# Setup, scatter table and first prologue merged into the first attention block, the atoms' products in its second slot of scores

## What is computed

```python
x = x + tanh(g_xattn[0]) * rope_cross_attention(layernorm(x), ctx)      # 32 heads of 16
x = x + tanh(g_ffn[0])   * mixture_of_16_experts(layernorm(x))          # top 4
x = x + tanh(g_xattn[1]) * normed_cross_attention(layernorm(x), ctx)
x = x + tanh(g_ffn[1])   * sparse_delta_layer(layernorm(x))             # W and 8 deltas, top 2
```

## Time and profile before

| | us |
|---|---|
| median of 3 runs | 2079.18 (2077.33 to 2079.27) |
| the profiled execution | 2078.01 |
| its span in the trace | 2076.2 |
| mean granted clock of TensorE, as a share of 2.4 GHz | 0.953 |

### The profile page before, as it was taken

One profiled execution on the slowest core, in us unless ns is written; L12 is line 12 of the kernel. 1 busy time (PEld: TensorE's weight loads), 2 busy tenths in 40 slices (PEclk: granted clock), 3 DMA queues, 4 the chain that ended last, 5 costly groups with the idle time before them and its releaser, 6 DMA issues. The chain is left out here.

```text
span 2076.2 us, 38678 instructions
## 1 busy us (share of the span) xinstructions
PE 1843.8 (89%) x11487; PEld 1407.4 (68%) x11487; DVE 1178.7 (57%) x2618; ACT 928.4 (45%) x2627; POOL 962.2 (46%) x1012
## 2 busy tenths in 40 slices
PE   4599999999986999999999999995689999886992
PEld 1355665666554999999999999993356566555881
DVE  5566677767653776433333343334777777764445
ACT  4267676767652332233333333321366666641110
POOL 1487777876741066133433334332455555311660
PEclk9899999999987999999999999998899999996996
DMA  8578877787755426589999988544345454529657
GB/s 324 183 233 271 255 224 249 248 261 229 224 159 171 155 63 206 165 248 269 296 319 280 281 247 248 114 77 112 83 94 117 105 115 101 131 94 374 233 163 273
DMA packets 233756, 414.81 MB, mean 200 GB/s; under 512 B 44289, under 2 KB 121225, under 8 KB 228242
## 3 DMA queue, kind: packets, MB, share of 16 engines
q1 hardware_dynamic: 167194, 324.12, 49.0%
q0 software_dynamic: 30592, 62.54, 13.1%
q10 hardware_dynamic: 35776, 25.69, 4.0%
HBM read 211.97 MB, written 157.82 MB: 178 GB/s over the span
## 5 line engine op out<-in xcount | busy, mean ns | idle before, releaser
L705 ACT ACTIVATE a_P<-a_SC,a_nm 128x256 f32<-128x256 f32 x512 | 235.9, 473 | 130.4 <-DVE a_nm L607 129.6
L1227 POOL DMA_INDIRECT b_y_rows<-b_ysb,b_entry x79 | 124.4, 1575 | 334.6 <-ACT b_ysb L1375 182.2
L607 DVE TENSOR_REDUCE a_nm<-a_SC 128x2 f32<-128x512 f32 x256 | 164.8, 685 | 142.2 <-PE a_SC L838 142.2
L570 POOL TENSOR_TENSOR a_praw<-a_praw,a_phigh 128x704 f32<-128x704 f32 (+2 forms) x126 | 191.8, 1523 | 10.3
L1479 DVE TENSOR_TENSOR b_xl<-b_XT,b_xh 128x512 fp32r<-128x512 f32 x97 | 67.1, 692 | 216.8 <-ACT b_xh L1381 216.3
L849 PEld LDWEIGHTS a_T<-ident,a_P 128*128 128x128 f32 x1024 | 118.5, 144 | 79.6 <-issue 46.3
L849 PE MATMUL a_T<-ident,a_P 128*128 128x128 f32 x1024 | 145.3, 280 | 20.9 <-DVE a_PT L619 17.8
L568 POOL CAST a_phigh<-a_praw 128x704 fp32r<-128x704 f32 (+2 forms) x126 | 111.3, 883 | 100.2 <-DMA a_praw<-in_L_ffn_wd 34.2
L2212 ACT ACTIVATE c_P<-c_SC,c_nm 128x240 f32<-128x240 f32 x256 | 115.7, 457 | 75.8 <-DVE c_P L2084 75.8
L1485 DVE TENSOR_TENSOR b_al<-b_AT,b_ah 128x384 fp32r<-128x384 f32 x111 | 61.9, 558 | 150.0 <-ACT b_ah L1386 150.0
L1375 ACT ACTIVATE b_ysb<-b_Y 128x512 f32<-128x512 f32 x79 | 47.2, 598 | 222.2 <-PE b_Y L1322 212.3
(11 more groups left out here) (494 smaller groups left out, 4923.6 us busy)
## 6 DMA issues: line engine op xcount, KB each, us to landing
w_parts<-a_phigh SPq DMA_DIRECT2D x72, 352.0 KB, 3.7
w_parts<-a_praw SPq DMA_DIRECT2D x72, 352.0 KB, 4.1
b_wh<-w_parts SPq DMA_DIRECT2D x18, 1216.0 KB, 10.3
b_wl<-w_parts SPq DMA_DIRECT2D x18, 1216.0 KB, 13.8
c_q<-c_qT SPq DMA_DIRECT2D x64, 256.0 KB, 4.2
c_k<-c_kT SPq DMA_DIRECT2D x124, 128.0 KB
b_wh<-w_parts SPq DMA_DIRECT2D x18, 704.0 KB, 4.7
b_wl<-w_parts SPq DMA_DIRECT2D x18, 704.0 KB, 7.3
```

The lines of the kernel that those rows point to most:

```text
L570: eng.tensor_tensor(raw[:, 0:k * m], raw[:, 0:k * m], r32(high[:, 0:k * m]), ALU.subtract).then_inc(plow_done, 1)
L607: eng.tensor_reduce(nm[:, g % 4, j, :], SC[j][:, :].rearrange("p (t k) -> p t k", t=BT), AX.X, ALU.max, negate=True).then_inc(topped, 1)
L705: e = eng.activation(Pr[:, i, t, :], SC[j][:, t * S:(t + 1) * S], ACT.Exp, bias=nm[:, g % 4, j, t:t + 1], accum_out=den[:, h, t:t + 1])
L1227: eng.indirect_dma_start(out=y_rows, out_offset=bass.IndirectOffsetOnAxis(ap=entry[:, r, 1:2].bitcast(U32), axis=0), in_=ysb[:, v % RING, ...
```

## The change

`setup` and `scatter_tables` go; all they do now stands in `rope_attention`'s block and its slots. Core of the diff:

```diff
-        setup(nc, core, g_xattn, g_ffn)
-            scatter_tables(nc, core, x, W, atoms, atom_weights, importance, mask_idx, table)
+        rope_attention(nc, core, x, ctx_1024, fside_BxSx2_0, *attn0, g_xattn, g_ffn,
+                       (W, atoms, atom_weights, importance, mask_idx), table, split)
+    FIRST_ITEMS_AT = {-15: ("X0", "X1"), -14: ("Q0",), -13: ("K0",), -12: ("Q1",), -11: ("q0a",), -10: ("K1",),
+                      -9: ("V0", "k0a"), -8: ("q1a",), -7: ("V1",), -6: ("q0b", "k0b"), -5: ("q1b",), -3: ("k1a",), -2: ("k1b",), 1: ("E",), 4: ("S0",), 6: ("S1",),
...
-    SPLIT_AT, NRAW, NHIGH = -6, 4, 3
+    FIRST_COLUMN_AT = {8: 0, 10: 1, 12: 2, 14: 3}
+    SPLIT_AT, SPLIT_END, NRAW, NHIGH = 10, END + 1, 4, 3
+    SECOND_TOKENS = -1
+    EARLY_AT = {-15: (1,), -14: (2,), -13: (3,), -12: (4,), -10: (5,), -8: (6,), -6: (7,)}
+    MATCH_AT, MATCHES = 1, 2
+    KEPT_IN = (0, 1, 2, 3, 4, 0, 1, 2)
```

```diff
+            def late_loads(s):
+                if s == -7:
+                    for i in range(3):
+                        q = slice(4 * i + 4, 4 * i + 8)
+                        eng.dma_start(core.X[:, q, :], xf[:, q, :]).then_inc(x_in[i + 2], 16)
+                if s == -4:
+                    for i in (3, 4):
+                        eng.wait_ge(wide_out[i], WIDE_OUT[i])
+                    eng.dma_start(row_i[:, :, :].rearrange("p c q -> p (c q)"), mask_idx.partition_broadcast(P)).then_inc(rows_in, 16)
+                if s == 2:
+                    filled(eng, (0, "E"))
...
```

```diff
+            eng.wait_ge(ident_set, 2)
+            eng.wait_ge(W_in, 16)
+            for k in range(KD):
+                turn_maps(k)
...
+                        for i in range(CH):
+                            m = eng.matmul(w[:, E * (CH * h + i):E * (CH * h + i + 1)], at_[k, P * i:P * (i + 1)], eaT[k, :],
+                                           start=True, stop=True)
```

```diff
+                if s == 2:
+                    place_weights()
+                if s == 5:
+                    place_half(0)
+                if s == 7:
+                    place_half(1)
```

More of the change, by code:

```diff
@@ new lines, in angles @@
+        eng.wait_ge(adone, a.now)
+        eng.tensor_scalar(U, U, MAGIC, None, ALU.add).then_inc(adone, a.inc())
+        eng.wait_ge(adone, a.now)
+        eng.tensor_scalar(U, U, -MAGIC, None, ALU.add).then_inc(adone, a.inc())
+        for part in (HI, LO):
+            eng.wait_ge(adone, a.now)
+            eng.tensor_scalar(V, U, -part, None, ALU.mult).then_inc(adone, a.inc())
+            eng.wait_ge(adone, a.now)
+            eng.tensor_tensor(A, A, V, ALU.add).then_inc(adone, a.inc())
+        eng.wait_ge(adone, a.now)
@@ L365, in items, with split_before, due @@
         return [(b, n) for b, n, i, j in pieces(s) if j == TERMS.get(n[0], 1)]
[L367 to L369 removed]
+    def split_before(s):
+        return min(max(0, (s - SPLIT_AT) * split.count // (SPLIT_END - SPLIT_AT)), split.count)
+    def due(s, first, others):
+        return [(b, at[s - PAIRS * b]) for b, at in ((b, others if b else first) for b in range(B)) if s - PAIRS * b in at]
     number = {}
@@ new lines, in place_weights @@
+            def place_weights():
+                w = bank((0, "E"))
+                filled(eng, (0, "E"))
+                eng.tensor_copy(wgt[:, :, :], w[:, C * E:2 * C * E].rearrange("p (e c) -> p c e", e=E)).then_inc(pseq, cp.inc())
+                eng.wait_ge(pseq, cp.now)
+                eng.tensor_tensor(wgt[:, :, :], wgt[:, :, :], w[:, 0:C * E].rearrange("p (c e) -> p c e", e=E),
+                                  ALU.mult).then_inc(*freed((0, "E")))
+                is_freed(eng, (0, "E"))
+                cur = wgt[:, :, :]
+                left = rest[:, :].rearrange("p (c e) -> p c e", e=E)
+                for i in range(NP):
+                    if i:
+                        eng.wait_ge(pseq, cp.now)
+                    if i == NP - 1:
+                        eng.tensor_copy(parts[:, :, i, :], cur).then_inc(parts_ready, 1)
+                        break
+                    eng.tensor_copy(parts[:, :, i, :], cur).then_inc(pseq, cp.inc())
+                    eng.wait_ge(pseq, cp.now)
+                    eng.tensor_tensor(left, cur, parts[:, :, i, :], ALU.subtract).then_inc(pseq, cp.inc())
+                    cur = left
```

548 lines of the change are left out of this document (288 added, 260 removed).

## The result

The changed kernel takes **2107.0 us** (median of four runs, 2098.1 to 2113.0) against 2078.3 us before in the same session (2077.3 to 2079.3): ratio 1.0136, 95% interval 1.0102 to 1.0170. It is slower by 28 us, where 2053 was forecast. The profiled execution took 2110.2 us with a span of 2108.2, against 2078.0 and 2076.2.

A forecast was written before the change was run, and what follows sets the result against it. It took the scatter block as bound by transfers and the prologue by a chain of engines, with TensorE busy 378 of 398.5 us in steady slots. 2078.0 - 46 + 20 + 1 = 2053 us; 8-in-10 range 2038 to 2070.

The forecast's parts named there:

- Part 1: Up to the first maxima: the merged prologue brings them from 93.9 to 48 us, -46 us.
- X0: Prologue: normed tokens end about 13 us, so X0's transposes stand at about 13 instead of 62.08.
- 5 us are hidden beside the b halves: Prologue: the exchange, issued in slot -8 behind q1a, has its 5 us hidden, so scores come at 46.7.
- GpSimd's angles: Prologue: twelve small operations, some 5 us, ending about 10 us.
- Rival 1: Prologue slower than its parts: widening not hidden, or angles, code or transfers late; scores near 60 give 2066; chance 0.18.
- Part 2: First ten intervals between maxima: work added there makes 65.7 us against 45.4, +20 us.
- scales in slot 8: VectorE in slot 8: twenty small operations, 3.7 us, in an interval of 7.5 us.
- E: Third interval: item E, 64 recorded pairs of load and matmul on TensorE, taken at 10 us, 7.4 to 22.
- row_i: Indices for the comparisons: 2 MB queued behind the table, landing near 60 us; VectorE might wait 4 us.
- Part 3: Steady slots and block's end: extra pieces stay hidden, two in slot 128 cost 0 to +3, taken as +1 us.
- add at most 6% to that, 0.17, still hidden by 1.2 of room: Steady slots: 126 pieces in 119 slots add 0.17 us to GpSimd's 2.9 a slot, hidden.
- The one for "slower": Dense slots: TensorE's clock stays low, +2.7 us a slot, 2094 at 15 more slots; chance 0.04.

The follow-up runs named there:

- e3: The change with the last scales in slot 6 instead of slot 8; the twenty operations take 3.6 us, the interval 5.68 us instead of 14.49.
- e15: The change with GpSimd's pieces from slot 12 on and its columns in slots 11 to 14; the twenty scale operations take 4.7 us instead of 11.0.
- e11: The change with five raw and four high-part buffers, last scales in slot 6, and E split over slots -9, -5 and -2; 2063.8 us.
- e13: e11 with the load of `row_i` ahead of the 3 MB of x in slot -7; 2061.0 us.
- e1: The change with one piece of weights a slot and the seven surplus pieces at the block's end; 2090.6 us, steady stretch 463.6 us.
- e9: The change with a fifth buffer for raw pieces, high parts keeping three; steady stretch 463.9 us.
- e16: e13 with the seven slots of two pieces moved to the fifth slot of each sequence; 2052.7 us.
- e14: The change itself run once more; ratio 1.0136 to the kernel before, 1432.9 us behind its block.
- e5: The change with E in slot -2, `place_weights` in slot 0 and `row_i` loaded earlier; first scores 7.9 us later, eleventh maxima 8.5 us earlier.

## Why the prediction was wrong

**Part 1, -46: measured -41.4.** The order of events was right, ScalarE's widening was done at 45.9 us as worked out, and the first maxima at 52.5 missed the band of 44 to 52 by half a microsecond. What failed is the step that the exchange's "5 us are hidden beside the b halves". Its eight transfers were issued from 39.99 on, 6.37 us long, and among table halves and x they landed only at 51.3; the scores waited 6.4 us for them. GpSimd's last angle, X0 and the first scores (start us, us, engine line op):

```profile
15.60 0.40 POOL L266 TENSOR_SCALAR rt_ang<-rt_ang 128x256 f32<-128x256 f32 x1
18.26 1.97 PE L1024 MATMUL a_W<-ident,a_xn 128*128 128x128 f32 x8 [4.44 <-POOL a_xn L616]
51.28 0.58 PE L1114 MATMUL a_SC<-a_kT,a_qT 32*128 32x256 f32 x2 [6.40 <-DMA a_qS<-a_qT]
```

Two things made it late. The chain began late: GpSimd's angles took 9.8 us (6.19 to 16.00) where 5 were put, and a first clearing of V, 1.4 us, for which the prediction has no term, stood between them and the normed tokens, so X0 stands at 18.26 and not at 13. Rival 1 had named the angles. And from its first issue to the scores the exchange took 11.3 us, against 6.9 in the kernel before. Either alone would leave the scores near 46 or 47, an estimate from these rows; no run separates them.

**Part 2, +20: measured +33.1.** Of the 12.8 us too much, 7.0 are the scales in slot 8 (14.49 instead of 7.5) and 4.1 the interval with E; the rest are differences of both signs, none above 2.0. "Scales in slot 8: twenty small ones, 3.7" took the price of an idle neighbour. The trace of before had the opposite: the "one of them slow" of the prediction lasts 1.88 us, to 58.38, while GpSimd clears V, to 58.35.

```profile
56.50 1.88 DVE L123 TENSOR_SCALAR a_llw<-a_llw 128x16 f32<-128x16 f32 x1
```

```profile
55.66 2.69 POOL L536 MEMSET a_V<- 128x1536 f32 x2
```

Rows 6 had a pair of engines in each other's way as well; the prediction read it as GpSimd being slowed by VectorE and asked nowhere what GpSimd does to VectorE, nor what GpSimd would run in slot 8. e3 and e15 show it. E was put at 10 us and took 14.7: the pairs cost 0.22 us since the clock was low, 0.12 where it is full (e11), so the range held and the value taken, 10, was that of neither level. Also `row_i`, said to land near 60, landed at 72.3, because its issue stood behind 4.3 and 6.0 us of other issues on SyncE and behind 3 MB of x. It cost nothing as long as E was longer, and 7 us as soon as it was not (e11, e13).

**Part 3, +1: measured +31.4** (29.8, 0.6 and 1.0), and this turns the sign: parts 1 and 2 as measured still leave a gain of 8.3 us. The failed step is "add at most 6% to that, 0.17, still hidden by 1.2 of room". It counted GpSimd's work and not the rings. The prediction named two pieces in one slot, and what they do to SyncE's queue can be read from the kernel: a load waits for the store of four pieces earlier, and a piece is stored one slot behind its split. Two in a slot take away exactly that slot of lag. The waits were in the trace of before, 66.0 us in 62 times, so the ring had no slack to lose; the prediction has no term for it. e1 (463.6 us without doubles) and e9 (463.9 with a fifth buffer) show it from two sides.

**The rivals.** The one for "slower", at 0.04, was TensorE's clock in dense slots. The low level is part of each long interval, 1.97 instead of 1.04 us for eight transposes, but it follows the gap and does not make it. Its price was off too: 6.71 against 3.60 us makes 7.3 us of the 3.94, not 6.8, so 3.2 us a slot and 8 slots to use up the gain. None of the four had the rings, so 93% stood on one side for want of one row.

**What is left of the sum.** e16, with the three causes taken out, is at 2052.7 where 2053 stood. That is luck and no proof of the sum, for it is another kernel and its terms are others. In its profiled execution, 2047.4, they are -41.0 up to the first maxima, +11.8 to the seventeenth, -1.2 behind them. So the merger pays most of what part 1 hoped for once the rest is paid for with buffers and places; for the kernel as changed the forecast was wrong by 54 us.

**The last 8.9 us** lie behind the block, where the code is the same. Over the twenty executions of the table this stretch took from 1429.4 to 1442.7 us, and the change itself 1439.1 and then 1432.9 (e14). So some 6 of the 8.9 us are the spread of that stretch. That the change adds nothing there isn't shown: 1430.2 before is one execution.

## What to carry to other kernels

When work is packed denser into the slots of a software pipeline, count the lag of each ring of buffers and not only the busy time: two in one slot use up a slot of lag, and where the trace already shows the queue waiting for its own stores, there is none to spare. One more buffer, in memory that was dead at the time, brought the block's end 24 to 28 us forward here (e9 against the two profiled executions of the change).

A chain of small operations costs its idle price only where the neighbour engine idles: look at what GpSimd runs in the slot where they are put. And a transfer that lands in time because something else is late will be the next wait when that is mended: move both.

## What the runs showed of the hardware

- Beside an operation of GpSimd some VectorE operations of 0.17 us last up to 1.63 us in the change, five of seven to the end of GpSimd's, also where they have a single input (L87, L90). In the kernel before one with a single input lasts 1.88 us beside a clearing, while four with two inputs in SBUF beside the same clearing (L114 to L120) take 0.18. Others are spared: the copy from PSUM at 300.80 us took its 0.68 beside GpSimd's cast at 300.81, and 109 reciprocals of four numbers in the steady stretch took 0.158 to 0.170.
- The mean granted clock was 0.95 from 46 to 48 us and 0.50 from 48 to 50 in e5, though TensorE was busy 2.0 of 2 us in both with products of 8 columns (it had idled for 0.54 us ahead of 46); in the change it stayed at 0.98 up to 50 us with TensorE idle since 45. The same pairs ran at 1.00 at 36 and at 44 us in e11.
- A pair of weight load and product of 8 columns (64 rows, float32, as recorded) takes 1.95/16 = 0.12 us at full clock and 6.99/32 = 0.22 at the low level.
- The same code behind the block took from 1429.4 to 1442.7 us from one execution to another, and 1439.1 and 1432.9 in two of the same kernel.
